# Attention over 8192 keys: in each key tile TensorE forms the second-pass scores ahead of the first-pass scores

## The reference, cut to what matters

```
q = heads(LN(x) @ W_Q + b_Q);  k = heads(ctx @ W_K + b_K);  v = heads(ctx @ W_V + b_V)   # 16 heads of 32
attn = softmax(q @ k.T / sqrt(32))            # per head: 512 queries by 8192 keys
x = x + (attn @ v, heads side by side) @ W_O + b_O
```

## Time and profile before

| | |
|---|---|
| three runs | 3616.47, 3619.70, 3619.74 us |
| profiled execution | 3621.52 us; its span (first to last instruction) 3619.5 us |
| TensorE matmuls busy | 3498.1 us, 97% |
| VectorE, ScalarE, GpSimd busy | 68%, 54%, 48% |
| attention of layer 0, heads 0 to 15 | starts at 697.4 us of the span |
| attention of layer 1, heads 0 to 15 | starts at 1983.0 us of the span |

### The profile page before, as it was taken

How to read it: one execution, slowest core, us unless ns; L and a number is a source line. 1 busy time by engine, 2 the same in 40 slices (tenths; PEclk the granted TensorE clock), 3 DMA queues, 4 the chain that set the end, 5 groups by cost and what they waited for, 6 DMA issues and landing times. The chain is left out here.

```text
span 3619.5 us, 46469 instructions
## 1 busy us (share of the span) xinstructions
PE 3498.1 (97%) x17788; PEld 2346.5 (65%) x17788; DVE 2470.7 (68%) x3461; ACT 1957.9 (54%) x3024; POOL 1736.3 (48%) x524
## 2 busy tenths in 40 slices
PE   8999999999999999988999999999999896999999
PEld 6788787755555555446876555555554485888887
DVE  3222344477777777357996787777774565999998
ACT  2122322366666666634972766666666322777786
POOL 2222222299999999600000999999997220100001
PEclk9999999899999999998998999999999998999999
DMA  7777776633333333046977433333330101999998
GB/s 274 253 245 233 237 241 208 192 80 91 93 91 83 92 87 88 3 179 217 364 306 237 122 93 91 83 93 87 90 85 18 53 1 78 348 381 372 376 373 303
DMA packets 249725, 627.92 MB, mean 173 GB/s; under 512 B 43889, under 2 KB 138129, under 8 KB 194977
## 3 DMA queue, kind: packets, MB, share of 16 engines
q1 hardware_dynamic: 210720, 551.54, 46.9%
q10 hardware_dynamic: 36864, 67.13, 5.0%
q0 software_dynamic: 1920, 6.29, 0.5%
HBM read 487.92 MB, written 136.87 MB: 173 GB/s over the span
## 5 line engine op out<-in xcount | busy, mean ns | idle before, releaser
L790 DVE TENSOR_REDUCE maxima<-psum 128x1 f32<-128x512 f32 x2048 | 1256.4, 682 | 358.7 <-PE psum L785 358.7
L928 ACT ACTIVATE pt<-psum 128x512 f32<-128x512 f32 x2048 | 1037.2, 624 | 525.8 <-PE psum L807 523.3
L942 POOL TENSOR_TENSOR exp_sums<-pt 128x1536 f32<-128x1536 f32 x216 | 753.4, 3488 | 282.6 <-ACT pt L928 277.0
L785 PE MATMUL psum<-ks,first_q 96*128 96x512 f32 x2048 | 845.1, 414 | 1.5 <-DMA ks<-k_parts 0.6
L807 PE MATMUL psum<-qs,ks 97*128 97x512 f32 x2048 | 826.2, 409 | 14.3 <-ACT pt L928 10.8
L944 POOL TENSOR_TENSOR exp_sums<-exp_sums,pt 128x1536 f32<-128x1536 f32 x216 | 754.8, 3494 | 17.0
L823 PE MATMUL psum<-pt,vs 128*32 128x512 f32 x4096 | 651.8, 598 | 1.9
L825 PE MATMUL psum<-exp_sums,constants 128*32 128x512 f32 x1344 | 621.8, 599 | 0.0
L1643 DVE TENSOR_TENSOR moe_cut<-moe_raw,moe_cut 128x2048 fp32r<-128x2048 f32 x244 | 557.0, 2290 | 58.5 <-ACT moe_cut L1639 52.7
L785 PEld LDWEIGHTS psum<-ks,first_q 96*128 96x128 f32 x2048 | 390.5, 191 | 283.9 <-issue 147.5
L1639 ACT CAST moe_cut<-moe_raw 128x2048 fp32r<-128x2048 f32 x244 | 468.9, 1923 | 57.5 <-PE psum L97 46.1
(11 more groups left out here) (336 smaller groups left out, 4534.7 us busy)
## 6 DMA issues: line engine op xcount, KB each, us to landing
moe_raw<-in_moe_w SPq DMA_DIRECT2D x244, 1024.0 KB, 8.1
ks<-k_parts SPq DMA_DIRECT2D x384, 256.0 KB, 4.6
k_parts<-kparts ACTq DMA_DIRECT2D x256, 256.0 KB, 4.4
cx<-in_ctx SPq DMA_DIRECT2D x32, 1024.0 KB, 6.1
vs<-v_heads SPq DMA_DIRECT2D x32, 1024.0 KB, 5.2
v_heads<-vrow SPq DMA_DIRECT2D x25, 1024.0 KB, 5.1
late_context<-cparts SPq DMA_DIRECT2D x28, 512.0 KB, 11.6
late_parts<-late_context SPq DMA_DIRECT2D x28, 512.0 KB, 4.6
```

The lines of the kernel that those rows point to most:

```text
L785: pe.matmul(self.c.bank[self.FIRST_BANK + k % self.FIRST_ROOM], self.first_q[s][:, t * P:(t + 1) * P], self.ks[s][part][0:3 * DH, at:at + ...
L790: dve.tensor_reduce(self.maxima[:, h % 2, i % TT, i // TT:i // TT + 1], self.c.bank[self.FIRST_BANK + k % self.FIRST_ROOM], X, ALU.max).th ...
L928: act.activation(self.pt[:, self.slot(h, t), :], self.c.bank[self.SECOND_BANK + n % self.SECOND_ROOM], ACT.Exp).then_inc(*self.exp.up())
L942: engine.tensor_tensor(to, self.pt[:, first + lo:first + hi, :], self.pt[:, later + lo:later + hi, :], ALU.add).then_inc(*signal.up())
```

## The change

In the tile loop of `head(h)` one call moves from behind the first-pass matmuls of the tile to ahead of them. The waits at a head's start, `turn_early`, `output_early`, `finish_head` and `weigh` keep their places. Nothing is added or removed, and the lists of the other engines stay as they are.

```
--- before.py
+++ after.py
@@ -840,10 +840,10 @@
             pe.wait_ge(*self.row_in[h % 2].at(TT * (h // 2 + 1)))
             pe.wait_ge(*self.q_in[h % 2].at(3 * (h // 2 + 1)))
             for t in range(KT):
+                second_on_pe(h, t)
                 for k in range(begun, self.first_to(h, t)):
                     self.first_on_pe(pe, k)
                 begun = self.first_to(h, t)
-                second_on_pe(h, t)
                 if h + 2 == HEADS and t in self.TURN_AT:
                     turn_early(self.TURN_AT.index(t))
                 if h + 1 == HEADS and t in self.PRODUCTS_AT:
```

## The result

22 runs of the changed kernel have a median of 3624.3 us, 22 of the kernel before in the same comparison 3618.4 us; the ratio is 1.0017, 95% interval [1.0011, 1.0024]. So the new order is slower by 6.2 us, between 4.0 and 8.7. Forecast was +7.1 us (3619.7 to 3626.8). The forecast of the time itself lies 2.5 us above the measured 3624.3; 1.3 of them come from its base, the median of three runs, which the 22 runs put at 3618.4.

What follows compares the result with a forecast made beforehand. TensorE's own list and the short stops in it were taken to bound the kernel. Adding 6.6 us at tile 20 and 0.5 us at head 14's turn to 3619.7 gave 3626.8 us, range 3618 to 3633.

Steps and rivals of the forecast that it cites:

- What the swap does to a block: Between weighings, VectorE starts one matmul later, ScalarE one earlier; bank stops keep their length: 0 us.
- Where it doesn't cancel: Tile 20's weighing waits for VectorE's chain from tile 12; stop grows 0.14 to 0.38 us, 28 x 0.235 = 6.6 us.
- The second place: First `turn_early` of head 14: reductions from tile 48 start 0.24 us later, 2 x 0.235 = 0.5 us.
- Steps at nothing: Next head's `neg_max`, key loads, GpSimd's additions and ScalarE's exponential after a copy have slack or are absorbed: 0 us.
- the exponential behind the copy: ScalarE's tile 12 exponential, needed by second score 15: 0 to 0.05 us a head (1.4 us over 28), taken as 0.
- The switch into weighing: About 208 switches, now behind a first-pass matmul: 0.33 us as before, no difference; bounds -19 to +15 us.
- Rival A: Switch into weighing cheaper behind a 96-row matmul, saving 19 us at its low bound: 3608 us; chance 6%.
- B: Switch costs up to 0.07 more, or exponential behind the copy stops TensorE: +1.4 to +15, say 3634 us; 8%.
- Rival C: VectorE's chain doesn't end `divided`, its delay is made up, or TensorE ignores the new order: 3619.7 us; 8%.
- D: Appears only in the chances, half to slower and the rest to same; the given text doesn't define it.
- Sum: Whole kernel: 6.6 + 0.5 = 7.1 us added, 3619.7 to 3626.8 us.
- the 0.2% bound: Limit by which faster, same and slower are told, 7.2 us; the forecast lay on it, a hair toward same.

Runs made afterwards that it cites:

- experiment 6: Kernel before, old order, with VectorE finishing a head behind tile 16's reduction and forming negated maxima behind tile 56's; ratio 0.9973 against before.
- experiment 1: Kernel before with the second-pass score ahead of the first-pass one at tile 12 alone; ratio 1.0018 against before.
- (3): Kernel before with the second-pass scores of tiles 12 and 13 both ahead of tile 12's first-pass score; ratio 1.0028 against before.
- experiment 8: Changed kernel with the old order kept at tiles 12 to 17; ratio 1.0005 against the kernel before.
- experiment 4: Changed kernel with VectorE finishing a head behind tile 16's reduction instead of 17's; ratio 0.9982 against the kernel before.
- experiment 7: Changed kernel with the old order kept at tiles 12 and 13; ratio 0.9996 against the kernel before.
- experiment 2: Changed kernel with the old order kept at tile 12 alone; ratio 0.9992 against the kernel before.
- 12: Kernel before, old order, with VectorE's head finish behind tile 16's reduction, negated maxima behind 56's, output-bias addition behind 37's; ratio 0.9962 against before.
- experiment 10: Changed kernel with VectorE's head finish behind tile 16's reduction, negated maxima behind 56's, output-bias addition behind 38's; ratio 1.0013 against the kernel before.
- 5: Kernel before, old order, with VectorE finishing a head behind tile 16's reduction instead of 17's; ratio 0.9993 against before.

## Why the prediction was right

- **What the swap does to a block.** Right: six of the seven block kinds are unchanged to 0.011 us. That a stop for a bank stays in length showed in the block up to tile 56, whose 0.18 us (experiment 6) were the same in both orders.
- **Where it doesn't cancel.** Right in place and size: +0.232 us a head against 0.235, and 28 x 0.232 = 6.5 us. Shown by one swapped tile (1), the double dose (3), the way back (8) and the shorter chain (4).
- **The second place**, the turn: +0.23 us by blocks in either layer, 0.5 us together as forecast. By starts of second scores head 14 is 0.69 longer; 0.46 are its two places, and the other 0.235 is the measure, as said at the table. Counted from first score matmul to first score matmul head 14 grows from 52.66 to 53.12, the 0.46 and nothing else.
- **Steps at nothing.** The weighing of tile 1 and the start of a head didn't move; the exponential behind the copy cost nothing in the new order. In experiment 7, where second score 14 moves up and the one of tile 12 doesn't, small stops of 0.02 us appear at tiles 15 and 16, the size of the bound.
- **The switch into weighing**, the term without a row: behind a second-pass matmul it takes 0.324 to 0.328 us (before, all tiles but 20), behind a first-pass one 0.324 to 0.327 (after, tiles 1, 29, 38 and 47). At tiles 11 and 56 of after, behind a first-pass matmul that had itself stopped for its bank, it is 0.37 and 0.43, and the blocks still have their old lengths. Rival A falls by that, and the first half of B.
- **Rival C** falls by experiments 1 and 8. **D**: the stretch of half clock in head 0 of layer 0 is 20.5 us long in before's trace, 17.1 in after's, but 20.5 again in experiment 8's and 10.2 in that of experiment 1, so it doesn't go with the order. It is part of what spreads the runs.
- **Sum.** 6.5 + 0.5 = 7.0 us by blocks and 7.2 by heads, against 6.2 [4.0, 8.7] by the clock. That the clock agrees so well is in part luck. In experiment 2 the trace has heads 1 to 14 longer by 3.1 us and the clock the kernel shorter by 2.9 [0.0, 6.2]; in 6 it is 3.5 against 9.8 [4.7, 14.5] shorter, in 12 it is 8.7 against 13.8 [9.1, 18.5]. Outside these heads the traces differ by more than the effect: 437 to 443 us between the attentions, 54.1 to 57.1 in head 15. Whether a kernel keeps such a difference in all its runs I don't know, with one trace of each. The proof is in the blocks.
- **Slips that change nothing.** By the rivals' own chances slower, same and faster add up to 48, 46 and 6%, not 49, 44 and 7, and the switches are 2 x (14 x 7 + 5) = 206, not 208. The chance was put on both sides of the 0.2% bound; the ratio fell just inside it, while its interval excludes no change.

What the prediction didn't see: it took the chain for a thing that starts at tile 12 and runs by itself. Experiments 2 and 7 show that later matmuls in it, those of tiles 13 and 17, have less slack than the 0.23 us of one matmul, so that keeping its beginning alone in the old order recovers only part.

## What to carry to other kernels

Swapping two equal instructions cost nothing here on the engine that issues them. It moved one of the engines fed by them one instruction later and the other one earlier, 0.47 us against each other. Look for the wait that one of these feeds by a gapless chain, because only there did the shift come out (and, in experiment 10, where the length of an instruction hung on the other engine), and shorten that chain rather than choose the order. Where a reader engine was idle before each burst, waits for its buffers cancelled in the swap. In runs that scatter by 0.5%, compare block lengths in the trace, to 0.01 us, and use the clock only as a coarse check; and count a stretch from the same point of the work in both orders, not from an instruction that the change itself moves.

## What the runs showed of the hardware

A VectorE addition with both inputs in SBUF (128x512) that starts while GpSimd runs a TENSOR_TENSOR ends 0.55 us after GpSimd's instruction: 1.02 us long in before, 1.22 in experiment 4, 1.61 in 5 and 3.62 in 10, according to where in GpSimd's 3.5 us it fell, and 0.68 where it fell on a boundary. GpSimd pays too: the instruction that begins while the addition still runs lasts 3.80 us instead of 3.48 (experiment 10). VectorE's reductions out of PSUM beside the same GpSimd instructions keep their pace of 0.60 us. The Trainium skill (SBUF — State Buffer, Who interferes with whom) says that a VectorE instruction with two SBUF inputs contends with a GpSimd one that reads SBUF, and that the port pair that the two share is an exclusive lock. The traces agree in that the addition doesn't end before GpSimd's instruction has; the 0.55 us is what they add. A swap of two matmuls of 0.235 us thus cost 1.7 us a head in heads 1 to 3 of experiment 10.
